# Attention and pooling for eight batches on one core: own steps for the first two and the last three batches

## What is computed

```python
# layer 0: x attends with queries from the side input, 16 heads of 16
query = seq2 + b_self
key   = concatenate([seq1 + b_prev, seq2 + b_self], 1)
value = concatenate([seq1, seq2], 1)
q, k, v = heads(query @ Wq + bq), heads(key @ Wk + bk), heads(value @ Wv + bv)
score_prev = where(mask, einsum('bhqd,bhkd->bhqk', q, k[:, :, :l1]) * SCALE, -inf)
score_self = (q * k[:, :, l1:]).sum(-1, keepdims=True) * SCALE
weights = softmax(concatenate([score_prev, score_self], -1))
attn = weights[..., :-1] @ v[:, :, :l1] + weights[..., -1:] * v[:, :, l1:]
x = x + (merge_heads(attn) @ Wo + bo)
# layer 1: masked pooling over the rows
scores = tanh(x @ W1 + b1) @ v1
p = softmax(where(mask_of(kind), scores[:, None, :], -1e30))
x = x + (p @ x) / count(mask)[..., None]
```

## Time and profile before

| | us |
|---|---|
| median of 3 runs | 289.73 |
| lowest, highest | 289.36, 295.17 |
| the profiled execution | 288.65 |
| its span in the profile | 287.0 |
| PE busy in the span | 239.8 (84%) |
| DVE, ACT, POOL busy | 185.5, 157.1, 76.2 |

### The profile page before, as it was taken

The page is one execution under the profiler, slowest core; times in us unless marked ns, Lnnn a source line. Parts: engine busy times, 40 slices in busy tenths (PEclk is TensorE's granted clock), DMA queues, the critical chain, the costliest instruction groups (busy, mean ns, idle before and its releaser), DMA issues.

```text
span 287.0 us, 6087 instructions
## 1 busy us (share of the span) xinstructions
PE 239.8 (84%) x2100; PEld 188.8 (66%) x2100; DVE 185.5 (65%) x384; ACT 157.1 (55%) x297; POOL 76.2 (27%) x87
## 2 busy tenths in 40 slices
PE   2986897699799999999999999999998768765643
PEld 1985776377577877777778687778776545534522
DVE  2659755266577777777976777688858667334231
ACT  4351323376477657674867486667666465671220
POOL 8035021031115113411431152126102403214101
PEclk9999579599999999999999999999999889999757
DMA  6379437822963394449525961783187110200001
GB/s 152 96 247 244 100 110 214 195 76 89 237 140 134 105 224 127 144 146 204 160 86 171 193 193 37 207 163 112 37 228 146 39 39 0 78 0 8 29 2 37
DMA packets 28021, 35.50 MB, mean 124 GB/s; under 512 B 4440, under 2 KB 24416, under 8 KB 28000
## 3 DMA queue, kind: packets, MB, share of 16 engines
q1 hardware_dynamic: 27360, 33.12, 43.9%
q0 software_dynamic: 640, 2.10, 2.0%
HBM read 20.26 MB, written 14.69 MB: 122 GB/s over the span
## 4 chain that ended last, share of the span: by engine, by line
PE 65%; DVE 13%; DMA 7%; issue 7%; ACT 4%; SPq 2%; POOL 0%; ACTq 0%; DVEq 0%
PE ps_any L1001 21%; PE ps_any L1055 11%; PE ps_max L1029 9%; PE ps_any L1008 7%; PE ps_exp L1042 4%; PE ps_any L1220 3%; DMA k_rows<-k_spill 3%; PE ps_any L1155 3%; DVE s_max L802 2%; DMA k_spill<-k_lo 2%; DVE x1t_lo L885 2%; DVE pool_pt_lo L952 2%; DMA x_sb<-in_x 2%; DVE bv_cast L769 2%; PE ps_any L1115 2%
## 5 line engine op out<-in xcount | busy, mean ns | idle before, releaser
L802 DVE TENSOR_REDUCE s_max<-ps_max 128x4 f32<-128x1024 f32 x64 | 78.0, 1219 | 25.2 <-PE ps_max L1029 25.2
L530 ACT ACTIVATE pt<-ps_exp 128x1024 f32<-128x1024 f32 x64 | 65.6, 1025 | 50.8 <-PE ps_exp L1042 50.2
L1029 PE MATMUL ps_max<-k_rows,q_rows 49*128 49x256 f32 x256 | 33.7, 342 | 11.2 <-DMA k_rows<-k_spill 6.5
L1055 PE MATMUL ps_any<-pt,v_aug 128*32 128x256 f32 x512 | 35.5, 396 | 1.2 <-ACT pt L530 1.2
L1029 PEld LDWEIGHTS ps_max<-k_rows,q_rows 49*128 49x128 f32 x256 | 20.2, 194 | 21.9 <-issue 10.8
L488 POOL TENSOR_TENSOR attn<-num,rden 128x256 f32<-128x256 f32 x16 | 9.6, 622 | 66.2 <-DVE rden L942 66.2
L1042 PE MATMUL ps_exp<-q_rows,k_rows 51*128 51x256 f32 x256 | 26.8, 287 | 0.0
L1055 PEld LDWEIGHTS ps_any<-pt,v_aug 128*32 128x32 f32 x512 | 13.7, 111 | 11.8 <-issue 2.7
L477 POOL TENSOR_TENSOR prod_lo<-prod,prod_hi 128x512 fp32r<-128x512 f32 x8 | 10.3, 1283 | 42.2 <-ACT prod_hi L626 42.2
L1042 PEld LDWEIGHTS ps_exp<-q_rows,k_rows 51*128 51x128 f32 x256 | 20.3, 191 | 1.1 <-issue 0.9
L1001 PE MATMUL ps_any<-st_hi,w_hi 128*128 128x256 f32 x64 | 20.9, 326 | 0.0
(11 more groups left out here) (145 smaller groups left out, 612.7 us busy)
## 6 DMA issues: line engine op xcount, KB each, us to landing
q_rows<-q_spill SPq DMA_DIRECT2D x32, 192.0 KB, 4.4
k_rows<-k_spill SPq DMA_DIRECT2D x32, 192.0 KB
q_spill<-q_hi SPq DMA_DIRECT2D x16, 256.0 KB, 2.5
k_spill<-k_hi SPq DMA_DIRECT2D x16, 256.0 KB, 2.5
s_sb<-in_fside_BxSxS SPq DMA_DIRECT2D x8, 256.0 KB, 3.3
x_sb<-in_x SPq DMA_DIRECT2D x8, 256.0 KB, 2.8
q_spill<-q_lo SPq DMA_DIRECT2D x8, 256.0 KB, 2.2
k_spill<-k_lo SPq DMA_DIRECT2D x8, 256.0 KB, 3.2
```

Of the source, the lines that this page charges most:

```text
L530: nc.scalar.activation(pt[:, 2 * j % 8:2 * j % 8 + 2], ps_exp[:], ACT.Exp).then_inc(p_ready, 1)
L802: nc.vector.tensor_reduce(s_max[:, j // MJ, :, :, j % MJ].rearrange("p t e -> p e t"), ps_max[:], AX.X, ALU.max).then_inc(max_found, 1)
L1029: last = pe.matmul(ps_max[:, e, t], q_rows[par][rows, j, P * t:P * t + P], k_rows[par][rows, j, :], start=True, stop=True)
L1055: last = pe.matmul(bank[32 * c:32 * c + 32, 0, :], v_aug[par][:, t, h, :], pt[:, h % 8, t, :], start=(t == 0), stop=(t == KB - 1), skip_gr ...
```

## The change

The order is no longer coded in each engine's `period` but in a table of steps (`REGULAR`), with the same places as before, and a second table (`MOVED`) with own places for batches 0, 1, 6 and 7 and two steps of batch 5. `at(name, i, k, s)` answers which batch's step is due in step s of a period. Periods 3 to 6, the loop, keep their order on every engine. The core of the diff:

```diff
+REGULAR = {
+    "TS": (0, 1), "TX": (1, 1), "Q": (2, 1), "K": (5, 1), "KS": (6, 1), "KS'": (7, 1), "VS": (9, 1), "SS": (10, 1),
...
+MOVED = {
+    0: {"max1": (0, 1), "max2": (0, 2), "max3": (0, 3), "group_max0": (0, 4), "MT0": (0, 5), "mt_copy0": (0, 5),
+        "max4": (0, 4), "max5": (0, 5), "max6": (0, 6), "max7": (0, 7), "group_max1": (0, 8),
+        "MT1": (0, 9), "mt_copy1": (0, 9),
+        "exp0": (0, 8), "exp1": (0, 9), "exp2": (0, 10), "exp3": (0, 11),
+        "exp4": (0, 12), "exp5": (0, 13), "exp6": (0, 14), "exp7": (0, 15),
+        "p_arg": (0, 9), "p_self": (0, 13), "vs_p": (0, 14),
+        "PV0": (0, 11), "pv_copy0": (0, 12), "PV1": (0, 12), "pv_copy1": (0, 13), "PV2": (0, 14),
+        "pv_copy2": (0, 15), "PV3": (1, 0), "pv_copy3": (1, 1),
+        "NAT": (1, 2), "num": (1, 3), "attn": (1, 3), "x_bo": (1, 5),
+        "AT": (1, 4), "at_hi": (1, 5), "at_lo": (1, 5), "WO": (1, 6), "x1": (1, 7), "x1_hi": (1, 8), "x1_lo": (1, 8),
+        "hidden": (1, 8), "X1T": (1, 9), "x1t_hi": (1, 10), "x1t_lo": (1, 10), "Z": (1, 11), "tanh": (1, 12),
+        "SB": (1, 13), "masked": (1, 14), "pool_p": (1, 14), "PT": (2, 0), "pt_hi": (2, 1), "pt_lo": (2, 1),
+        "PO": (2, 2), "PO'": (2, 2), "out": (2, 3), "store": (2, 3)},
+    1: {"TS": (-1, 13), "st_hi": (-1, 14), "st_lo": (-1, 14), "TX": (-1, 14), "xt_hi": (-1, 15), "xt_lo": (-1, 15),
+        "Q": (-1, 15), "q_copy": (-1, 15), "q_lo": (-1, 16), "K": (-1, 15), "KS": (0, 0), "KS'": (0, 1),
+        "k_hi": (0, 1), "prod": (0, 2), "prod_hi": (0, 3), "prod_lo": (0, 3), "VS": (0, 3), "SS": (0, 5),
+        "V": (0, 6), "V'": (0, 8), "ss_copy": (0, 6), "vs_copy": (0, 6), "v_copy": (0, 10)},
+    5: {"PT": (7, 13), "pt_hi": (7, 14), "pt_lo": (7, 14), "PO": (7, 15)},
+    6: {"exp3": (7, 1), "exp4": (7, 4), "exp5": (7, 5), "exp6": (7, 6), "exp7": (7, 7),
+        "PV1": (7, 2), "pv_copy1": (7, 3), "PV2": (7, 6), "pv_copy2": (7, 7), "PV3": (7, 8), "pv_copy3": (7, 9),
+        "NAT": (7, 10), "num": (7, 10), "attn": (7, 11), "x_bo": (7, 12),
+        "AT": (7, 12), "at_hi": (7, 13), "at_lo": (7, 13), "WO": (7, 14), "x1": (7, 15),
...
+        "Z": (8, 3), "tanh": (8, 4), "SB": (8, 5), "masked": (8, 6), "pool_p": (8, 6),
+        "PT": (8, 8), "pt_hi": (8, 9), "pt_lo": (8, 9), "PO": (8, 10), "PO'": (8, 10), "out": (8, 11),
...
+    7: {"max1": (7, 1), "max2": (7, 2), "max3": (7, 3), "group_max0": (7, 4), "MT0": (7, 5), "mt_copy0": (7, 5),
...
+        "exp0": (7, 8), "exp1": (7, 9), "exp2": (7, 10), "exp3": (7, 11),
...
+        "PO": (9, 2), "PO'": (9, 2), "out": (9, 3), "store": (9, 3)},
+}
```

Batch 7 has the places of batch 0, seven periods later. Periods 0 to 2 then hold batch 0's chain earlier, and the banks of `ps_any` are taken in turn in periods -1, 0, 1 and from 7 on:

```diff
+            irregular = n < 2 or n >= B - 1
+            turn = (turn + 1) % BANKS
+            TAKEN_BANKS[take] = turn if irregular else BANK[take[0]]
```

`x1`, `x1_hi` and `x1_lo` get two buffers. On SP the maxima of batch 0 are sent after all placements of batch 1, and in the last periods x is loaded again earlier:

```diff
                 if live(*prv):
-                    place_max(*prv, 1)
+                    if not is_first(*prv):
+                        place_max(*prv, 1)
+                    if last:
+                        load_again(*prv)
...
-                if live(*b):
+                if live(*b) and not is_first(*b):
                     place_max(*b, 0)
...
+                if is_first(*b):
+                    for g in range(NM):
+                        place_max(*b, g)
+                    load_again(*b)
```

The constants that DVE and PE made behind period -1 move into period 0, and their product goes into `ps_max` once the eight maxima are found:

```diff
+                    if is_first(i, k) and s == 9:
+                        cast_bv()
+                    if is_first(i, k) and s == 11:
+                        weight_lo(3)
+                        setup_pooling()
+                        dve.wait_ge(bv_product_ready, 1)
...
                 pe.wait_ge(bv_cast_done, 1)
+                pe.wait_ge(max_found, NJ)
```

More of the change, by code:

```diff
@@ L52 @@
+BANK = {
+    "PV0": 2, "TS": 1, "MT1": 0, "AT": 3, "TX": 2, "Q": 0, "WO": 1, "PV1": 3, "X1T": 0, "K": 2, "KS": 1, "Z": 0,
+    "PV2": 3, "MT0": 0, "SB": 2, "VS": 1, "SS": 0, "V": 2, "PV3": 3, "PT": 0, "NAT": 1, "NAT'": 0, "PO": 3,
+}
 BANKS = 4
@@ new lines, in at, with takes @@
+        def at(name, i, k, s):
+            step, offset = REGULAR[name]
+            due = []
+            if s == step and live(i, k + offset):
+                if not isinstance(i, int) or name not in MOVED.get(2 * i + k + offset, {}):
+                    due.append((i, k + offset))
+            if isinstance(i, int):
+                due += [(m // 2, m % 2) for m in sorted(MOVED) if MOVED[m].get(name) == (2 * i + k, s)]
+            return due
+        def takes(n):
+            for s in range(STEPS):
+                for name in TAKES:
+                    for i, k in at(name.strip("'"), n // 2, n % 2, s):
+                        yield name, 2 * i + k
@@ new lines, in bank_free @@
+        def bank_free(name, i, k):
+            if isinstance(i, int):
+                take = (name, 2 * i + k)
+                earlier = [t for _, t in TAKEN[:[t for _, t in TAKEN].index(take)] if TAKEN_BANKS[t] == TAKEN_BANKS[take]]
+                if not earlier:
+                    return None, None
+                other, m = earlier[-1]
+                reader, done = TAKES[other]
+                return sems[reader], PER_BATCH.get(reader, 1) * m + done
+            idx = [other for other, _ in REGULAR_TAKES].index(name)
+            period = k - REGULAR_TAKES[idx][1]
+            for back in range(idx - 1, idx - 1 - len(REGULAR_TAKES), -1):
+                other, offset = REGULAR_TAKES[back]
+                if BANK[other] == BANK[name]:
+                    reader, done = TAKES[other]
+                    kk = period + offset - (back < 0)
+                    return sems[reader], count(i, kk, PER_BATCH.get(reader, 1), done)
@@ L979, in _ @@
+                    for j in range(NJ):
+                        for c in at(f"max{j}", i, k, s):
+                            max_of(*c, j)
             weight_lo(0)
@@ new lines, in period @@
+                    for c in at("AT", i, k, s):
+                        bank = take_bank("AT", *c)
+                        pe.wait_ge(attn_done, count(*c, 2, 2))
+                        transposed(bank, attn).then_inc(at_ready, 1)
+                    for c in at("WO", i, k, s):
+                        bank = take_bank("WO", *c)
+                        pe.wait_ge(at_hi_done, count(*c, 1, 1))
+                        pe.wait_ge(at_lo_done, count(*c, 1, 1))
+                        if isinstance(i, int):
+                            pe.wait_ge(w_lo_ready, 4)
+                        products(bank, at_hi, at_lo, 3, False).then_inc(wo_ready, 1)
@@ L1227, in _ @@
+                    for c in at("PO'", i, k, s):
+                        pooled(*c, banks["PO"], 1).then_inc(po_ready, 1)
             pe.wait_ge(ident_ready, 1)
```

766 lines of the change are left out of this document (377 added, 389 removed), and 9 rows, old and new, of the table REGULAR.

## The result

The changed kernel took 296.86 us (median of 4 runs, 294.93 to 298.58), the kernel before beside it 289.55 us; the ratio is 1.029 (95% interval 1.023 to 1.034). The change made the kernel slower, by 7 to 8 us. The forecast was 285.9 us with a range of 280.5 to 291.5: wrong in sign and outside the range. The profiled execution took 295.41 us, span 293.7.

A forecast was written before the change was run, and what follows sets the result against it. PE was taken to bound the middle periods (busy 26.9 of 27.7 us), hand-offs and a DMA chain the rest. Head +3.6 and tail -7.4 us gave -3.8, from a median of 289.73 to 285.9 us, range 280.5 to 291.5.

The forecast's parts named there:

- the head: From the start to batch 3's first max scores: +3.6 us, 109.9 for 106.3; bounds -1 and +10.
- (a): End of period -1, before batch 0's first max scores: K waits for v_copy behind other copies, +2.2 us.
- (b): Period 0, batch 0's first max scores to batch 1's: eight maxima, then eight exps, 27.6 us where 24.5 stand.
- my own case: Whole kernel: head +3.6, tail -7.4, forecast 285.9 us; own range 283 to 288.5, chance 0.48.
- my second rival: Period 0 and some of period 7: clock at 1.2 GHz, 6.9 us for period 0, total 293; chance 0.13.
- one of my signs of being wrong: Period 0: the clock standing at 0.5 all through it would show the forecast wrong.
- The third rival: Period 0: batch 0's maxima land behind batch 1's placements, exps start 3 us late, total 289; chance 0.10.
- (c): Period 1, batch 1's first max scores to batch 2's: less work but in a chain, k_rows last; 26.5 us.
- (d): Period 2, up to batch 3's start: first half shrinks, DMA chain limits the second; 25.7 us for 27.8.
- (e) to (g): From period 7's start to the end: 5.8 us gained to NAT, 1.4 to AT, 0.2 to Z; -7.4 us.
- The third limit: Ends of periods 0 and 1: DMA chain from transposed first maxima to next batch's k_rows, 11.2 and 10.9 us.

The follow-up runs named there:

- e12: e9 with batch 0's first maxima placed between the two groups of batch 1's rows; 293.02 us, ratio 1.017.
- e13: Changed kernel with all mends: e12's fillers, constants and early placing, e10's spill order, e4's attn order; 288.04 us, ratio 0.998.
- e9: Changed kernel with bias constants back behind period -1 and smaller dummy-matmul fillers only where PE waited; 296.40 us.
- e5: Changed kernel with only the bias constants (cast, product, pooling set-up) put back behind period -1; 297.25 us.
- e10: Changed kernel with k's spill issued ahead of the first maxima's placing in the periods after period 0; 293.28 us, ratio 1.018.
- e4: Changed kernel with q_lo of batch 2 one step later, so attn of batch 0 comes first on GpSimd; 296.81 us.
- e2: Changed kernel with the head's change alone, the end as in the kernel before; 306.37 us, ratio 1.061.
- e14: Changed kernel with only batch 0's first maxima placed early, between the two groups of batch 1's rows; 297.05 us.
- e8: Tail-only kernel (e1) with k's spill issued ahead of the first maxima's placing in every period; 278.30 us, ratio 0.963.
- e1: Changed kernel with the head's parts put back as before, so the tail's change alone; 281.87 us, ratio 0.975.
- e11: Kernel before with only k's spill issued ahead of the first maxima's placing; 283.36 us against 288.31, ratio 0.983.
- e3: Changed kernel with 74 dummy matmuls put into the waits of period 0 and before AT in period 1; 297.61 us.

## Why the prediction was wrong, point by point

The tail came as forecast; the head lost 14.1 us where 3.6 were forecast. The 10.5 us between them are 2.6 us less than forecast in period -1, and 6.4, 3.9, 1.1 and 1.7 us more in periods 0, 1, 2 and 3; period 3 I had left out.

**(a) The end of period -1** was forecast 2.2 us longer and came 0.4 us shorter. The mechanism was there: K waits 2.15 us for v_aug behind ACT's four copies. But PE left 1.2 GHz at about 9.5 us in this execution, and at about 19 in the one of before. In e12, where it left late again (between 17.9 and 18.9), and in e13 the first max scores came at 31.8 and 31.7, of which 1.0 is the bias product: some 2.8 us above the 27.9 of before, near the forecast. But these two are the exception: of the twelve kernels with a changed head ten left 1.2 GHz by 11.5 us, and began batch 0 at 26.9 to 29.3. My working had no term for this, and whether the early rise is chance or comes with the change isn't shown.

**(b) Period 0** is the step that failed: 34.0 us for 27.6. I wrote that the rest of batch 1's preparation, PV and the output bias hide in the gaps, and took the rounds at the durations of the earlier trace rows, which are rows at 2.4 GHz; my own case has nothing in its sum for the clock. The terms of the failure are those of my second rival, which I priced at 6.9 us for a low clock all through period 0 and gave a chance of 0.13; a clock at 0.5 through period 0 was one of my signs of being wrong, and it stood there for some 23 of the 34 us. Measured: the maxima took 18.4 us, and 15.0 in e9 with the clock kept up, so 3.4 us. The exps took 15.6 us, and 12.6 in e12, so 3.0 us (the constants' product among it, which in e5 gave no gain when it left). Together they are the 6.4 us.

The same instructions of PE, DVE and ACT in period 0 took 31.8 us in e10 at a clock of 0.73, 34.0 in the changed kernel at 0.66, 34.8 in e4 at 0.61, and 37.6 in e2 and in e14 at 0.50; with fillers and without the constants it was 27.4 at 1.00. The prices of the rival are confirmed singly: I had 0.3 us a round and 1.0 for one with a PV; e5 against e12 gives 1.91 against 1.63 and 2.59 against 1.71. Its sum was too low: 37.6 less 27.4 is 10.2 us for a low clock all through, with the constants' product among it, against my 6.9. It priced only the rounds, and at 1.2 GHz the work between them no longer hides: in the changed kernel PE works without a gap from 39.20 to 45.90, and the maxima round with half of VS and SS in it takes 3.80 us, in e9 2.12.

What was wrong besides is its chance, and my own rows spoke for it. In the kernel before, period 0 has 0.75 as its mean clock; the change takes the regular work out from between the rounds and lays rounds of maxima, where PE works 0.54 of 1.8 us, one behind the other. I read 12.2 of 16.6 us busy at 1.00 as a comfort, though period 0 "comes to about a half". How much the new order itself lowers the clock is only argued: the four kernels with the head of before have 0.66 (e8), 0.75, 0.85 (e1) and 0.91 (e11) in period 0, those with batch 0's own steps and no fillers 0.50 to 0.73.

The Trainium skill (TensorE: Matmul & The Clock Gate, Loop structure matters more than you think) says that the order of the loops decides whether matmuls stay at the full clock, and that a long wait for a DMA ahead of each puts them at half. The waits here are shorter, up to 2.19 us, and for DVE and ACT. With that difference e12 agrees: the same rounds with 36 dummy matmuls in period 0's waits, and without the constants, stand at 1.00 and take 6.6 us less than at 0.66. Of that 3.8 us reached the total (296.86 to 293.02, intervals that overlap), as period -1 was longer in e12 and the later periods kept their waits.

**The third rival**, the maxima of batch 0 late behind batch 1's placements, was real too, and I had it at 0.10. At the low clock it cost nothing (e14); once the clock was mended, PE waited 3.13 us in e9, near the 3 us I gave it. In the traces the two cover one another, and I had treated the rivals as ways that exclude each other. In time this is less sure: the queue alone shows nothing (e14), and e3 was no clean test of the clock alone, but e9 mended it for the maxima, and its two shortest executions are as short as e12's.

**(c) Period 1** took 30.4 us for 26.5. Two waits weren't in my working: I had AT wait 2.5 us behind num and attn, and missed that q_lo of batch 2 stands ahead of attn on GpSimd (3.87 us in all); and at the end a reduce stands behind four operations of batch 0's pooling on DVE (1.85 us at batch 2's start). After the AT wait PE went at 1.2 GHz from 73 to 77.7. Neither mend alone gave it back: attn first 0.8 us (e4), the clock 0.5 (e12); in both the period then ended waiting for k_rows, 2.09 and 2.92 us. In e13, with both and k's spill first, it took 27.0. Which share is the spill's and which q_lo's isn't separated.

**(d) Period 2**: 26.8 us for 25.7, ending in the forecast wait for k_rows (2.77 us); 25.6 in e10, where that wait is gone. What the forecast left out is the echo: behind the wait the clock stood at 0.68 for 5 us and period 3, which I had called untouched "instruction by instruction", took 29.4 us and not 27.7. The wait isn't the whole of it: without it (e10) 28.8 stay.

**(e) to (g), the tail**: forecast -7.4, measured -7.4, and each of the steps within 0.6 us. That the same kind of change gains there I put down to batch 6's steps, which stand beside batch 7's rounds in period 7; no run separates it: PE is busy 29.7 of 35.7 us and its clock stays at 0.95, where period 0 has 0.66. And there is no next batch whose rows must be ready.

**The third limit** of my first part, the chain of 11.2 us from the transposed maxima to the next batch's k_rows, was misread. I took the transposed maxima for the chain's first cause. They were so only by SP's order: in e11 the spill of k_lo goes out as soon as k_lo is ready, and from the transposed maxima to batch 1 it is 9.2 us (38.33 to 47.54) where it was 11.2. That is where the kernel before had slack to give, and the one swap is worth 5 us by the medians.

**Can batch 0's own steps pay?** Not in any form tried. With every mend they reach 288.0 us, while the kernel without them reaches 278.3 (e8): as I read it, they trade a period of two overlapping kinds of rounds for two in series. That is 27.4 us of period 0 at the best clock against 19.3 in e11 (28.2 to 47.5, clock 0.91) and 23.3 in e8 (clock 0.66), and periods 1 and 2 give back none of it: 27.0 and 26.7 in e13, 23.9 and 27.7 in e11, 25.7 and 27.7 in e8. Another 3.5 us of the distance lie before period 0, which begins at 31.7 in e13 and at 28.2 in the other two. Batch 0's own steps with the mends but without batch 1's early preparation weren't run.

## What to carry to other kernels

Before rounds are laid end to end, take the durations at either clock that the new order may be granted, not only at that of today's rows, and price the work between the rounds too; where two suspected costs can cover one another, remove both at once before acquitting either. When a chain ends in a DMA, look at the queue for a transfer that was ready and stood behind another's wait: here one swap of two statements gave 5 us by the medians, more than the 3.8 us that the whole change was forecast to gain. And a change at both ends of a kernel is two changes: measured apart, one gained 8 us and the other lost 16.
